# Slot layer of a fused transformer: first weights read as 1152 contiguous floats per partition

## The reference, cut to what matters

```python
tok = _l2_normalize(xn)
sl = _l2_normalize(slots) * scale[:, None]
logits = jnp.einsum('sd,btd->bst', sl, tok)
dispatch_w = jax.nn.softmax(logits, axis=-1)
combine_w = jax.nn.softmax(logits, axis=-2)
y = jnp.einsum('btd,bst->bsd', xn, dispatch_w)
y = jnp.einsum('sio,bsi->bso', fc1_weight, y) + fc1_bias
y = jax.nn.gelu(y, approximate=False)
y = jnp.einsum('sio,bsi->bso', fc2_weight, y) + fc2_bias
out = jnp.einsum('bsd,bst->btd', y, combine_w)
```

## Time and profile before

| | us |
|---|---|
| median of three runs (lowest, highest) | 1700.4 (1700.31, 1700.66) |
| span of the profiled execution, first to last instruction | 1698.1 |
| PE busy | 1444.5 (85%) |
| DVE busy | 683.9 (40%) |
| ACT busy | 662.5 (39%) |
| POOL busy | 384.9 (23%) |

### The profile page before, as it was taken

The page is one execution under the profiler, slowest core; times in us unless marked ns, Lnnn a source line. Parts: engine busy times, 40 slices in busy tenths (PEclk is TensorE's granted clock), DMA queues, the critical chain, the costliest instruction groups (busy, mean ns, idle before and its releaser), DMA issues.

```text
span 1698.1 us, 31669 instructions
## 1 busy us (share of the span) xinstructions
PE 1444.5 (85%) x10300; PEld 1049.9 (62%) x10300; DVE 683.9 (40%) x2124; ACT 662.5 (39%) x2237; POOL 384.9 (23%) x464
## 2 busy tenths in 40 slices
PE   5899986796756778888899899699999999989994
PEld 3666664632212345666678799466765776789994
DVE  5557766511101376444423622433542423551113
ACT  1667663410000233777842122153663632213331
POOL 5212222300000122222200266220220200123441
PEclk8899996587778688999998899799999999889997
DMA  8434341679998400000003366200000200126553
GB/s 219 133 83 129 82 115 28 227 242 333 311 314 249 147 1 1 1 0 0 0 0 100 107 203 197 81 1 1 0 0 0 93 37 0 30 84 199 181 175 103
DMA packets 94439, 178.73 MB, mean 105 GB/s; under 512 B 35578, under 2 KB 54168, under 8 KB 92704
## 3 DMA queue, kind: packets, MB, share of 16 engines
q1 hardware_dynamic: 80144, 130.65, 26.1%
q10 hardware_dynamic: 7056, 30.67, 5.6%
q0 software_dynamic: 7136, 16.10, 3.1%
HBM read 150.39 MB, written 26.99 MB: 104 GB/s over the span
## 4 chain that ended last, share of the span: by engine, by line
PE 58%; issue 12%; DVE 12%; DMA 8%; ACT 6%; SPq 3%; POOL 1%; DVEq 0%; ACTq 0%; POOLq 0%
PE bank L1819 15%; DMA WM<-in_fc 7%; PE bank L2339 6%; PE bank L2325 4%; PE bank L1910 4%; PE bank L1922 3%; PE bank L1939 3%; PE bank L2329 3%; PE bank L1949 3%; PE bank L2000 2%; PE bank L1885 2%; PE bank L1992 2%; ACT ON L1604 2%; SPq L226 2%; PE bank L2256 1%
## 5 line engine op out<-in xcount | busy, mean ns | idle before, releaser
L1819 PE MATMUL bank<-XT,AREA 96*128 96x408 f32 (+1 forms) x640 | 239.1, 532 | 33.9 <-ACT XT L1558 16.6
L1819 PEld LDWEIGHTS bank<-XT,AREA 96*128 96x128 f32 (+1 forms) x640 | 122.1, 196 | 139.8 <-issue 99.8
L1910 PE MATMUL bank<-KZ,QT 128*102 128x102 f32 x1152 | 140.8, 262 | 9.0 <-ACT PB L1604 5.7
L664 POOL TENSOR_TENSOR PB<-PB,RCU 102x306 f32<-102x306 f32 x96 | 69.2, 720 | 318.5 <-DVE RCU L923 318.4
L648 POOL TENSOR_TENSOR RS<-VE,expo 102x4 f32<-102x4 f32 (+1 forms) x53 | 53.0, 1001 | 387.2 <-DVE VE L863 329.8
L1910 PEld LDWEIGHTS bank<-KZ,QT 128*102 128x102 f32 x1152 | 122.4, 174 | 27.2 <-issue 18.1
L2339 PE MATMUL bank<-WM,KZ 128*128 x660 | 118.2, 327 | 0.0
L2339 PEld LDWEIGHTS bank<-WM,KZ 128*128 128x128 f32 x660 | 105.7, 190 | 0.4
L1585 ACT ACTIVATE KZ<-bank,AREA 128x128 f32<-128x128 f32 x198 | 54.6, 374 | 121.8 <-PE bank L2329 121.8
L1922 PE MATMUL bank<-AREA,OT 128*102 128x192 f32 x384 | 88.9, 345 | 11.3 <-DVE SLOTS L1276 5.3
L1939 PE MATMUL bank<-PT,V 102*32 102x102 f32 (+1 forms) x1152 | 85.9, 270 | 14.5 <-DVE OT L933 12.3
(11 more groups left out here) (335 smaller groups left out, 2777.5 us busy)
## 6 DMA issues: line engine op xcount, KB each, us to landing
AREA<-in_fc SPq DMA_DIRECT2D x10, 1536.0 KB, 26.1
SLOTS<-in_m3w SPq DMA_DIRECT2D x33, 384.0 KB
WM<-in_fc ACTq DMA_DIRECT2D x5, 2304.0 KB, 19.5
WM<-in_fc SPq DMA_DIRECT2D x6, 1536.0 KB, 27.9
AREA<-in_fc ACTq DMA_DIRECT2D x4, 2304.0 KB, 20.6
SLOTS<-in_m1w SPq DMA_DIRECT2D x33, 256.0 KB
AREA<-pos_scratch SPq DMA_DIRECT2D x16, 459.0 KB
pos_scratch<-AREA SPq DMA_DIRECT2D x8, 913.5 KB
```

Of the source, the lines that this page charges most:

```text
L664: pool.tensor_tensor(p, p, scale, ALU.mult).then_inc(sem["probs_ready"], 1)
L1819: last = pe.matmul(dst, lhsT, rhs, start=n == 0, stop=n == len(pieces) - 1)
L1910: last = pe.matmul(psum[k][0:T, cols(j)], QT[:, tile, cols(bb)], KALL[:, unit % per_tile * (HEADS // per_tile) + tile, cols(bb)], start=Tr ...
```

## The change

The 192 x 768 first weights of a slot are read as 128 runs of 1152 floats, one for each partition. A run is one row and a half, so an even partition 2m holds row 3m and the first half of row 3m+1, an odd one 2m+1 the second half of row 3m+1 and row 3m+2. One DMA loads four slots; one of the seven places is split over three buffers and takes three DMAs. There are 32 loads of four slots (16 of first weights, 16 of second weights) in one order, `FIRST_AT` and `SECOND_AT`, through a ring of seven places. All are issued by SP: loads 0 and 1 at the start of the kernel, 2 to 6 after `attn0_done`, the others each when its place has been used. ACT issues none.

The first products run over half rows: for each of three chunks of 384 columns, four matmuls with 32 columns of inputs each. The first 16 of a slot's 32 output rows hold hidden columns 0 to 383 and the other 16 hold columns 384 to 767, so no output row is left over. For this the inputs lie in `YT` in four blocks a slot, with the partitions of the other parity multiplied by zero: POOL picks columns in `columns(g)`, PE makes two products of 128 columns a sequence, and ACT copies each twice with a mask (`parity`, made by DVE at the start). The bias product has 32 rows and 384 columns. Each quad has one gelu of 384 columns, three transposes and one copy by DVE. The bias goes from `fc1` through a new DRAM array `bias_rows` into `WM` at the start of the kernel, and SP waits in between. `CT`, `Y2T`, `PICK` move to other buffers. The second products keep their count and shapes, and read the two halves from 16 columns apart. The waits before the next layer's loads are named by the new ring's places. The diff, cut to its core:

```diff
-YTC = 3 * NSLOT // 2 * NB + 2 * NB
-QRING = 3
+PIECE = FF * D // 128
+BLOCKS = 4 * NB
+LOADS = 2 * QUADS
+FIRST_AT = tuple(max(2 * q - 1, 0) for q in range(QUADS))
+SECOND_AT = tuple(min(2 * q + 2, LOADS - 1) for q in range(QUADS))
+HALF_F = FF // 2
...
+        VALL = sb("V", [128, GB * HEADS * 64])
+        V = VALL[0:T]
...
-        YTF, YTH = SLOTS[:, 0:NSLOT * NB + NB], SLOTS[:, NSLOT * NB + NB:YTC]
-        YTS = [buf[:, 0:n * NB].rearrange("p (s b) -> p s b", s=n) for buf, n in ((YTF, NSLOT), (YTH, NSLOT // 2))]
-        BIAS, PICK = V[0:NSLOT, 0:FF], V[0:NSLOT, FF:FF + 32 * NSLOT]
-        Y2T = SLOTS[0:KD, YTC:YTC + 2048].rearrange("p (k s b) -> p k s b", k=2, s=NSLOT)
+        flat_q = QT[:].rearrange("p k t -> p (k t)")
+        flat_k = KZ[:].rearrange("p a k t -> p (a k t)")
+        YT = SLOTS[:, 0:NSLOT * BLOCKS].rearrange("p (s c) -> p s c", s=NSLOT)
+        BIAS = WM[:, 9 * PIECE:9 * PIECE + HALF_F]
+        PICK = ON[0][:, 0:32 * NB]
+        COLUMNS = sb("COLUMNS", [T, 2, GB, 128])
+        Y2T = XX[0:KD, 0:2048].rearrange("p (k s b) -> p k s b", k=2, s=NSLOT)
...
-        CT = SLOTS[0:NSLOT, YTC + 2048:YTC + 2048 + NB * T].rearrange("p (b t) -> p b t", b=NB)
+        CT = [buf[0:NSLOT, c:c + TG].rearrange("p (b t) -> p b t", b=GB)
+              for buf, c in ((AREA, 11 * PIECE), (AREA, 11 * PIECE + TG), (VALL, 2 * PIECE), (flat_q, FF + PIECE))]
...
-        def load_first(engine, q):
-            j, s = q % QRING, RING * q
-            rows = t["fc1"][s:s + RING].rearrange("s p k f -> (p k) s f")
-            engine.dma_start(FULL[j], rows[0:128]).then_inc(sem[f"fc1_loaded{j}"], 16)
-            for odd in range(2):
-                engine.dma_start(HALF[j][64 * odd:64 * odd + 64], rows[128:D, odd:RING:2]
-                                 ).then_inc(sem[f"fc1_loaded{j}"], 16)
...
+        HR = flat_of(QT, 128, 0, HALF_F)
+        YR = flat_of(QT, 128, HALF_F, HALF_F + D)
+        HS = flat_of(OT[0], 128, 0, HALF_F + NB)
+        run_of = lambda buf, c, n: buf[:, c:c + n * PIECE].rearrange("p (s c) -> p s c", s=n)
+        REGIONS = [[run_of(WM, 0, RING)], [run_of(WM, RING * PIECE, RING)], [run_of(flat_k, 0, RING)],
+                   [run_of(VALL, 0, 2), run_of(flat_q, FF, 1), run_of(SLOTS, NSLOT * BLOCKS, 1)],
+                   [run_of(AREA, 0, RING)], [run_of(AREA, RING * PIECE, RING)],
+                   [run_of(AREA, 2 * RING * PIECE, 3), run_of(WM, 2 * RING * PIECE, 1)]]
+        NR = len(REGIONS)
+        IN_AREA, IN_WM = (4, 5, 6), (0, 1, 6)
+        def weights_of(n):
+            return [run[:, r, :] for run in REGIONS[n % NR] for r in range(run.shape[1])]
+        def loaded_by(n):
+            return 16 * len(REGIONS[n % NR]) * (n // NR + 1)
+        def load_weights(engine, n):
+            if n in FIRST_AT:
+                s = RING * FIRST_AT.index(n)
+                rows = t["fc1"][s:s + RING].rearrange("s p k f -> s (p k f)")[:, 0:128 * PIECE].rearrange(
+                    "s (p c) -> p s c", p=128)
+            else:
+                s = RING * SECOND_AT.index(n)
+                rows = t["fc2"][s:s + RING].rearrange("s p f d -> p s (f d)")
+            first = 0
+            for run in REGIONS[n % NR]:
+                engine.dma_start(run, rows[:, first:first + run.shape[1], :]
+                                 ).then_inc(sem[f"slots_in{n % NR}"], 16)
+                first += run.shape[1]
+        def fills_of(r):
+            return len(range(r, LOADS, NR))
...
-            load_first(sp, 0)
-            load_second(sp, 0)
+            load_weights(sp, 0)
+            load_weights(sp, 1)
+            sp.dma_start(bias_rows, t["fc1"][:, KD, 0]).then_inc(sem["bias_stored"], 16)
+            sp.wait_ge(sem["bias_stored"], 16)
+            load(BIAS, bias_rows.rearrange("s (h f) -> (s h) f", h=2), "bias_loaded")
...
-            load(BIAS, t["fc1"][:, KD, 0], "bias_loaded")
-            for q in range(1, QRING):
-                load_first(sp, q)
-                load_second(sp, q)
-            for q in range(QRING, QUADS):
-                sp.wait_ge(sem[f"fc1_used{q % QRING}"], q // QRING)
-                load_first(sp, q)
-            sp.wait_ge(sem["fc1_used1"], fills_of(1))
-            sp.wait_ge(sem["fc2_used1"], fills_of(1))
-            sp.wait_ge(sem["fc1_used2"], fills_of(2))
-            sp.wait_ge(sem["fc2_used2"], fills_of(2))
+            for n in range(2, LOADS):
+                if n >= NR:
+                    sp.wait_ge(sem[f"slots_used{n % NR}"], n // NR)
+                load_weights(sp, n)
...
+            def columns(g):
+                if g > 0:
+                    pool.wait_ge(sem["columns_used"], g)
+                x = XND[g].rearrange("t b (m r) -> t b m r", r=3)
+                for half in range(2):
+                    pool.tensor_copy(COLUMNS[:, half, :, :].rearrange("t b (m r) -> t b m r", r=2),
+                                     x[:, :, :, 1 - half:3 - half]).then_inc(sem["columns_ready"], 1)
...
-            pool.wait_ge(sem["attn0_done"], 1)
-            for buf, n in ((YTF, NSLOT), (YTH, NSLOT // 2)):
-                pool.memset(buf[:, n * NB:(n + 1) * NB], 0.0).then_inc(sem["yt_padded"], 1)
...
+                columns(g)
+                if g + 1 < NG:
...
-            pool.wait_ge(sem["yt_padded"], 2)
-            pool.tensor_copy(PICK.rearrange("p (s c) -> p s c", s=NSLOT), ident[0:NSLOT, 0:NSLOT].unsqueeze(2).to_broadcast([NSLOT, NSLOT, 32])
-                             ).then_inc(sem["yt_padded"], 1)
-            pool.wait_ge(sem["fc1_used1"], fills_of(1))
-            pool.wait_ge(sem["fc2_used1"], fills_of(1))
-            pool.wait_ge(sem["fc1_used2"], fills_of(2))
-            pool.wait_ge(sem["fc2_used2"], fills_of(2))
+            pool.wait_ge(sem["dispatch_in"], NG)
+            for i in range(4):
+                rows = slice(32 * i, 32 * i + 32)
+                pool.tensor_copy(PICK[rows].rearrange("p (s c) -> p s c", c=NB),
+                                 ident[rows, rows].unsqueeze(2).to_broadcast([32, 32, NB])
+                                 ).then_inc(sem["pick_ready"], 1)
...
+            step(dve.tensor_reduce(parity[:], ident[:].rearrange("p (j two) -> p two j", two=2), AX.X, ALU.add))
...
-            def hidden_columns():
-                for half in range(2):
-                    k = at.bank(SBANKS)
-                    src = full(k)[:, 0:3 * 128].rearrange("p (f c) -> p f c", f=3)
-                    free(dve.tensor_copy(HS[:, 3 * half:3 * half + 3, :], src), k)
+            def hidden_columns(q):
+                k = at.bank(SBANKS)
+                src = full(k)[:, 0:HALF_F]
+                if q == 0:
+                    dve.memset(HS[:, HALF_F:], 0.0)
+                free(dve.tensor_copy(HS[:, 0:HALF_F], src), k)
...
-                src = [there[:, c:c + GB * n].rearrange("p (b s) -> p s b", b=GB)
-                       for c, n in ((0, NSLOT), (GB * NSLOT, NSLOT // 2))]
-                activation(YTS[0][:, :, g * GB:(g + 1) * GB], src[0], ACT.Copy)
-                free(activation(YTS[1][:, :, g * GB:(g + 1) * GB], src[1], ACT.Copy), k)
+                for half in range(2):
+                    src = there[:, half * GB * NSLOT:(half + 1) * GB * NSLOT].rearrange("p (b s) -> p s b", b=GB)
+                    for odd in range(2):
+                        c = NB * (2 * half + odd) + g * GB
+                        last = activation(YT[:, :, c:c + GB], src, ACT.Identity, scale=parity[:, odd:odd + 1])
+                free(last, k)
             at.first_banks()
             for q in range(QUADS):
-                for c0, c1 in ((0, 512), (512, FF)):
-                    k = at.bank(TBANKS)
-                    free(activation(HR[:, c0:c1], full(k)[:, 0:c1 - c0], ACT.Gelu), k)
-                ahead = q + QRING - 1
-                if QRING <= ahead < QUADS:
-                    act.wait_ge(sem[f"fc2_used{ahead % QRING}"], ahead // QRING)
-                    load_second(act, ahead)
+                k = at.bank(TBANKS)
+                free(activation(HR, full(k)[:, 0:HALF_F], ACT.Gelu), k)
...
-                for bb in range(GB):
-                    c = bb * NSLOT
-                    pe.matmul(p[:, c:c + NSLOT], x[:, bb, 0:128], DW[g % 2][:, bb, :], start=True, stop=True)
-                for bb in range(GB):
-                    c = GB * NSLOT + bb * NSLOT // 2
-                    for odd in range(2):
-                        last = pe.matmul(p[64 * odd:64 * odd + 64, c:c + NSLOT // 2], x[:, bb, 128:D],
-                                         DW[g % 2][:, bb, odd:NSLOT:2], start=True, stop=True)
+                pe.wait_ge(sem["columns_ready"], 2 * (g + 1))
+                for half in range(2):
+                    for bb in range(GB):
+                        c = (half * GB + bb) * NSLOT
+                        last = pe.matmul(p[:, c:c + NSLOT], COLUMNS[:, half, bb, :], DW[g % 2][:, bb, :],
+                                         start=True, stop=True)
...
             def into_slots(q):
```

(60 more changed lines are left out.)

65 lines of the change are left out of this document (24 added, 41 removed).

## The result

The changed kernel takes 1645.7 us (median of four runs, 1640.9 to 1654.3), the kernel before, timed beside it, 1700.5 (1700.3 to 1701.2): a ratio of 0.967, with a 95% interval of 0.964 to 0.971. The prediction was 1643, in a range of 1633 to 1668. The profiled execution took 1650.4 us, 4.6 above the median, with a span of 1648.6.

What follows compares the result with a forecast made beforehand. It took slot-weight transfers as the bound, slowed to 317 GB/s by 64-partition loads. Later dispatch, the 415 GB/s stream and a shorter end put the closing part 57.7 us earlier: 1700.4 - 57.7 = 1642.7, say 1643 us, 8-in-10 range 1633 to 1668.

Steps and rivals of the forecast that it cites:

- What bounds the stage: Slot stage: weight transfers set the time, with DMA engines full yet moving 317 GB/s; TensorE matters only at the two ends.
- the partition count is what differs: Slot stage: 64-partition loads ran at 259 GB/s, 128-partition loads at 393 to 418, with the same 3072-byte pieces.
- The start of the kernel: Kernel start: the parity reduction and SP's wait on the bias copy, in by 35 to 43 us, cost 0.
- The rate: Slot stage: the 25 remaining loads, 59.0 MB, stream at 415 GB/s in 142 us, ending at 498.7 us.
- rival 1: Slot stage: a long stream does not hold the peak; 356 GB/s, 166 us, gain 34, total 1667 us; chance 0.12.
- rival 3: Slot stage: all loads through SP's one queue run at 285 GB/s; stream 207 us, total 1707 us; chance 0.04.
- Dispatch: Four dispatch groups before the slot stage: PE +0.85 and ACT +0.66 us each, POOL +0.5 in all; about 6.5 us.
- First quad: Start of slot stage: SP issues the next load at 354.5 us, after a stage start at 347.7.
- Rival 2: Slot stage: PE stays at 1.2 GHz, 12.1 us a quad against 11.4 for loads; gain 19, 1681 us; chance at most 0.09.
- The end: After the last slot load: 1.5 us, then 4.1 of second products; closing part at 504.3 us instead of 562.04.
- the next layer's weights queue behind the last slot load: End of slot stage: what follows is unchanged, with 20 us of closing products over the next layer's weights.
- The total: Whole kernel: closing part 57.7 us earlier, taken from the median 1700.4, gives 1642.7, say 1643 us.

Runs made afterwards that it cites:

- control5: The changed kernel timed and profiled again with nothing altered: median 1641.5 us, ratio 0.964 to the kernel before.

## Why the prediction was right

**What bounds the stage**: right, the transfers. The step "the partition count is what differs", from FULL against HALF in the earlier trace rows, led to the right rate by a reason that was too coarse: the run over even and odd partitions shows that it's the half they lie in. A reader who takes "64 partitions are slow" from it would wrongly avoid a strided set.

**The start of the kernel**: cost 0, as forecast. The read of the bias, for which SP waited, was issued at 36.22 us, inside the 35 to 43 of the forecast, and the first stores of `pos_scratch` began at 47.64, against 48.00 before.

**The rate**: 415 forecast, 419 measured over 137.5 us, 421 over the middle 126. With that rival 1 (356) falls, and rival 3 (285, one queue); the run with two queues shows that their number makes no difference here. The figure of 358 from the Trainium skill's HBM Reference is thereby also out for this kernel. The same section says that a core streaming alone measures about 425; the prediction left that half out, and the trace agrees with it.

**Dispatch**: forecast 6.5 us; from the first dispatch product to the stage's start it took 40.14 us against 33.36 before, 6.8 more. The products took 3.69 (3.8 forecast), the four copies 1.57 (1.22 forecast): these follow each other by 0.39 us and not by the 0.28 of the earlier trace rows. The new copies take their scale from `parity`, the old ones had none; whether that is the difference no run here shows. POOL's column copies, 1.16 us a pair, don't appear in the chain of waits.

**First quad**: next load issued 6.6 us after the start (360.99 against 354.38), forecast 6.8.

**TensorE**: between 362 and 515 us it waited 19 times for a load, 2.1 us in the mean and 3.9 at most. Rival 2 (TensorE stays at 1.2 GHz and binds) falls: the mean granted clock was 0.86, and the run that gave it 20 us more work cost 1.7 us of stage.

**The end** is the term that was mis-sized. Forecast: closing part 156.6 us after the start (504.3 - 347.7). Measured: 160.5, 159.5 and 159.3. The step "the next layer's weights queue behind the last slot load" is where it failed. They were issued behind it but moved beside it: the last load was used 154.9 us after the start (509.29 - 354.38), against 152.5 forecast (500.2 - 347.7), and 151.2 with the wait added. The other 1.5 us are the half clock: from landing to closing 5.6 us, not 4.1, just above the 3.6 to 5.5 that the step allowed.

**The total**: forecast gain 57.7 us, measured 54.8 between the medians of the first runs, 56.1 and 60.7 in the two later pairs. In the profiled executions the span fell by 49.5: 60.3 from the stage, less 6.8 in dispatch, less 6.4 because dispatch began later, plus 2.4 behind the closing part. Not all of the 60.3 is the rate: 14.5 us stood between the last wait for a load and the closing part before, 5.6 now, since only second products follow the last load. The 6.4 are in no step of the prediction. They lie in code that the change leaves as it was, with a lower clock in places; in control5 the same stretch was 3.1 us earlier than before. So they count as spread, 13 us between runs of the changed kernel. The mechanism was right, but that 1643 came within 3 us of the first median is partly luck: the two terms that the profile checks, stage and dispatch, give 53.5 us and not 57.7, and the spread is larger than the difference.

## What to carry to other kernels

When DMA engines are full and the rate is low, look at which partitions each load writes, not only at the length of its pieces: loads that go to one half, one after the other, move 210 GB/s where the same bytes spread over both move 421, and a second queue mends only part of it. The last load of a stream needs protection from what is issued right behind it in the same queue: here it cost 8.6 us instead of 5.8. Where the runs spread by 13 us, a gain of 5 us is judged by the stage's own length in the trace, and a claim on the total needs many more runs.

## What was not expected

- A mixture of half loads and wide loads moves an eighth less than its parts would (244 against 280 GB/s, and 317 against 359 in the old stage).
- In the run whose loads have a source with a first dimension of two, the rate fell to 50 to 57 GB/s for long stretches: 9% of the whole time from an edit that kept bytes, destinations and count of loads.
- TensorE's clock was higher with more work: 0.82 to 0.86 in the changed kernel's stream, 0.92 with a third more products, and 1.9 us were lost on the last quad after a wait of 3.94 us that weren't after one of 1.24.
- The unaltered attention ahead of the stage began dispatch anywhere from 304.8 to 315.7 us, which is most of the spread in the spans, 1634.0 to 1648.6.
